# Sending expert rows to their tokens' places in a four-layer Trainium2 kernel, and summing over partitions with PE

## The reference

```python
# layer 2, x here is cond, 1024 x 256
probs = softmax(x @ gate_weight.T)                  # 8 experts
top_v, top_i = top_k(probs, 2);  top_v = top_v / top_v.sum(-1)
for each expert: gate, up = split(x @ gu.T);  y = (silu(gate) * up) @ dp.T
                 out += combine_w[:, e] * y
# layer 3
def weight_quant(w):                                # each of w1, w2, w3
    scale = 1.0 / clip(mean(abs(w)), EPS, None)
    return clip(round(w * scale), -1, 1) / scale
h = silu(bitlinear(x, w1)) * bitlinear(x, w2);  out = bitlinear(h, w3)
```

## Time and profile before

| what | us |
|---|---|
| three runs | 579.07, 580.73, 581.8 |
| median of them | 580.73 |
| the profiled execution's own time | 580.15 |
| its span | 578.4 |
| block loop, first gate_up to last `yb` | 338.7 to 498.6 |
| `yb` of the last block to the last add_y | 498.6 to 525.0 |
| layer 3 behind that | 525.0 to 578.4 |

### The profile page before, as it was taken

One profiled execution on the slowest core, in us unless ns is written; L12 is line 12 of the kernel. 1 busy time (PEld: TensorE's weight loads), 2 busy tenths in 40 slices (PEclk: granted clock), 3 DMA queues, 4 the chain that ended last, 5 costly groups with the idle time before them and its releaser, 6 DMA issues.

```text
span 578.4 us, 6195 instructions
## 1 busy us (share of the span) xinstructions
PE 409.8 (71%) x1772; PEld 265.3 (46%) x1779; DVE 400.1 (69%) x674; ACT 264.2 (46%) x638; POOL 244.4 (42%) x318
## 2 busy tenths in 40 slices
PE   0002599989799999866777259985998999410796
PEld 0001378756455656544556125643555565310464
DVE  4999938698999999997964717558376410153795
ACT  2411164678577777626784103321232323214694
POOL 4666600152985655852300223248156230264342
PEclk9999999999899999988896559999899999855898
DMA  7600000011011100000002197866888895130011
GB/s 245 267 0 1 1 19 1 2 36 38 0 36 38 35 3 19 2 0 1 2 1 74 53 368 260 288 221 228 302 266 323 304 319 195 47 91 27 0 37 36
DMA packets 19408, 60.48 MB, mean 105 GB/s; under 512 B 3024, under 2 KB 8400, under 8 KB 15792
## 3 DMA queue, kind: packets, MB, share of 16 engines
q1 hardware_dynamic: 17504, 54.99, 26.5%
q0 software_dynamic: 1872, 5.11, 3.7%
HBM read 54.98 MB, written 5.11 MB: 104 GB/s over the span
## 4 chain that ended last, share of the span: by engine, by line
PE 41%; DVE 32%; issue 10%; ACT 8%; DMA 4%; POOL 4%; SPq 0%; DVEq 0%; ACTq 0%; POOLq 0%
PE bank L1701 12%; PE bank L1721 6%; DVE fw L887 5%; DVE fw L875 5%; PE bank L1513 4%; DVE bw L878 3%; PE bank L1457 2%; DVE hx L1064 2%; PE bank L1391 2%; ACT rl L636 2%; DMA xb<-cond_rows,row_i 2%; PE bank L1393 2%; PE bank L1392 2%; POOL gy L480 2%; PE bank L1502 2%
## 5 line engine op out<-in xcount | busy, mean ns | idle before, releaser
L1701 PE MATMUL bank<-gu,xbT 128*128 128x512 f32 x184 | 88.4, 626 | 9.0 <-issue 8.1
L636 ACT ACTIVATE rl<-bank,cw 128x128 f32<-128x128 f32 x256 | 73.0, 379 | 38.1 <-DVE hx L1064 21.1
L1513 PE MATMUL bank<-hT,w2raw 128*128 128x512 f32 x128 | 67.8, 613 | 15.1 <-ACT hT L643 15.0
L1267 DVE TENSOR_TENSOR hm<-bank,sl 128x512 f32<-128x512 f32 x23 | 15.8, 687 | 73.6 <-PE bank L1701 42.3
L356 POOL TENSOR_TENSOR fw<-fw,bw 128x256 f32<-128x256 f32 x48 | 38.3, 798 | 53.6 <-DVE bw L878 53.6
L1403 PE MATMUL bank<-ident,GT 128*128 128x128 f32 x64 | 11.8, 340 | 66.4 <-DVE GT L892 45.6
L1701 PEld LDWEIGHTS bank<-gu,xbT 128*128 128x128 f32 x184 | 36.6, 201 | 47.7 <-issue 45.2
L887 DVE RECIPROCAL fw<-fw 128x256 f32<-128x256 f32 x32 | 55.8, 1743 | 0.6
L353 POOL TENSOR_TENSOR eu<-eu,kT 128x256 f32<-128x256 f32 x24 | 25.3, 1055 | 56.2 <-ACT eu L544 49.3
L1064 DVE SCALAR_TENSOR_TENSOR hx<-bank,rl 128x512 f32<-128x512 f32 x64 | 43.4, 680 | 7.7 <-ACT rl L636 7.3
L1721 PE MATMUL bank<-dn,hT 128*128 128x256 f32 x184 | 45.1, 388 | 3.3 <-ACT hT L759 0.7
(11 more groups left out here) (257 smaller groups left out, 878.6 us busy)
## 6 DMA issues: line engine op xcount, KB each, us to landing
gu<-in_gu SPq DMA_DIRECT2D x23, 1024.0 KB, 7.3
dn<-in_dn SPq DMA_DIRECT2D x23, 512.0 KB, 5.3
traw<-in_t SPq DMA_DIRECT2D x3, 1024.0 KB, 4.9
y_rows<-yb SPq DMA_DIRECT2D x23, 128.0 KB, 4.8
w1raw<-in_w SPq DMA_DIRECT2D x8, 256.0 KB, 3.4
w2raw<-in_w SPq DMA_DIRECT2D x8, 256.0 KB, 3.1
kT<-in_kt SPq DMA_DIRECT2D x4, 256.0 KB, 7.5
x<-in_x SPq DMA_DIRECT2D x2, 512.0 KB, 7.1
```

The lines of the kernel that those rows point to most:

```text
L636: ins = act.activation(rl[:, j % 2, e * P:e * P + P], bank[j][:, e * P:e * P + P], ACT.Relu, scale=cw0[:, t, 4 * eg + e:4 * eg + e + 1])
L1513: pe.matmul(bank[4 + o % 2][:], w2raw[:, slot, e, :], hT[:, e % 2, :], start=start, stop=stop, skip_group_check=True).then_inc(sem("y_done ...
L1701: ins = pe.matmul(bank[2 * (b % 2) + up][:], xbT[:, b % 2, k, :], gu[:, b % RING, k, up * I2:up * I2 + I2], start=(k == 0), stop=(k == KC ...
```

## The change

Four things. (1) `owner_i` is worked out before the slots instead of behind them, and SP holds back the weights of block 1 until the first gather has landed and those of block 2 until the second has. (2) The result of a block is no longer stored by SP in slot order but by POOL with an indirect DMA, each row to the place k * 1024 + token of its copy and token (`scatter_block`, two iterations behind); slots that no token has go to rows of their own. For that `tile_no` runs over 16 numbers instead of twice 8, `row_i` takes one DVE instruction more, and two more give `dest_i` (in place of `slot_i`). (3) Behind the loop SP reads `y_rows` back in order, 8 plain DMAs of 256 KB into a buffer of 2 MB that lies over the weights' buffers; DVE waits for two of them per pair of tiles. (4) The ternary sums over partitions are a PE matmul of one column with a matrix of ones, ahead of gate_up of blocks 4, 10 and 16, in a bank which the second half of that gate_up overwrites once DVE has read it; DVE's `ternary_round` moves from the end of its iterations 4, 10 and 16 to their start.

```diff
@@ SP
             for b in range(NB):
+                if 0 < b < RING:
+                    sp.wait_ge(sem(f"xb_in{b - 1}"), 16)
                 block_weights(b)
-                if b >= RING:
-                    block_out(b - RING)
                 if b in (1, 8, 14):
                     ternary_in((1, 8, 14).index(b))
-            for b in range(NB - RING, NB):
-                block_out(b)
+            sp.wait_ge(sem("y_out0"), 16 * ((NB + 1) // 2))
+            sp.wait_ge(sem("y_out1"), 16 * (NB // 2))
+            for b in range(B):
+                for k in range(2):
+                    rows_k = y_d[k * TOK + 2 * P * b:k * TOK + 2 * P * b + 2 * P, :]
+                    sp.dma_start(gy[:, b, k, :, :], rows_k.rearrange("(t p) c -> p t c", p=P)).then_inc(sem(f"gy_in{b}"), 16)
@@ POOL
+            def scatter_block(b):
+
+                pool.wait_ge(sem("y_ready"), b + 1)
+                pool.indirect_dma_start(y_d, bass.IndirectOffsetOnAxis(ap=dest_i[:, b:b + 1], axis=0), yb[:, b % 2, :], None
+                                        ).then_inc(sem(f"y_out{b % 2}"), 16)
...
             for b in range(NB):
                 if b + RING < NB:
                     gather_block(b + RING)
+                if b == 2:
+                    pool.wait_ge(sem("routed"), ROUTED["dest"])
+                if b >= 2:
+                    scatter_block(b - 2)
                 if b < 2 * NBLK:
                     late_sum(b // 2, 1 - b % 2, ("den", "num")[b % 2])
...
-                if b in (3, 9, 15):
-                    ternary_total((3, 9, 15).index(b))
                 if b in (6, 12, 18):
                     ternary_write((6, 12, 18).index(b))
@@ DVE
+            wide = [P, NBW, E2]
+            chain(dve.tensor_tensor(owner[:], slab[:].rearrange("p (j o) -> p j o", o=1).to_broadcast(wide),
+                                    nblk[:, 1, :].rearrange("p (o e) -> p o e", o=1).to_broadcast(wide), ALU.is_ge))
+            chain(dve.tensor_reduce(owner_f[:, 0, :], owner[:], AX.X, ALU.add))
+            dve.tensor_scalar(owner_i[:], owner_f[:, 0, :], float(E2 - 1), None, ALU.min).then_inc(sem("routed"), 1)
             chain(dve.tensor_tensor(nblk[:, 2, :], nblk[:, 1, :], nblk[:, 0, :], ALU.subtract))
...
-            dve.tensor_scalar(row_i[:], row_f[:, 1, :], 0.0, None, ALU.max).then_inc(sem("routed"), 1)
-            dve.tensor_copy(slot_i[:], slots[:, 0, :, :]).then_inc(sem("routed"), 1)
+            chain(dve.tensor_scalar(row_f[:, 2, :], row_f[:, 1, :], float(TOK), -float(TOK), ALU.is_ge, ALU.mult))
+            dve.scalar_tensor_tensor(out=row_i[:], in0=row_f[:, 1, :], scalar=0.0, in1=row_f[:, 2, :],
+                                     op0=ALU.max, op1=ALU.add).then_inc(sem("routed"), 1)
...
             def ternary_round(m):
                 dve.wait_ge(sem("tsum_ready"), m + 1)
-                chain(dve.tensor_scalar(ws[:, 15 + m:16 + m], ws[:, 12 + m:13 + m], 1.0 / (C * HID), 1e-5, ALU.mult, ALU.max))
+                dve.tensor_scalar(ws[:, 15 + m:16 + m], total_bank(4 + 6 * m), 1.0 / (C * HID), 1e-5, ALU.mult, ALU.max
+                                  ).then_inc(sem("tsum_read"), 1)
+                dve.wait_ge(sem("tsum_read"), m + 1)
@@ PE
+            def ternary_total(m):
+                pe.wait_ge(sem("tsum_part"), m + 1)
+                pe.matmul(total_bank(4 + 6 * m), ones[:], ws[:, 9 + m:10 + m], start=True, stop=True).then_inc(sem("tsum_ready"), 1)
...
                 wait(pe, sem("hm_ready"), b - 1)
+                if b in (4, 10, 16):
+                    ternary_total((4, 10, 16).index(b))
                 for up in range(2):
+                    if up and b in (4, 10, 16):
+                        pe.wait_ge(sem("tsum_read"), (4, 10, 16).index(b) + 1)
```

More of the change, by code:

```diff
@@ L45 @@
 ROUTED_SCALE = 2.5
-ROUTED = {"mk": 1, "lsub": 2, "owner": 3, "rows": 4, "slot": 5}
+ROUTED = {"mk": 1, "lsub": 2, "owner": 3, "rows": 4, "dest": 5}
 SUMMED = {"logit": 1, "place": 2, "rows": 3}
@@ L122, in build @@
         ones8 = sb("ones8", [P, E2])
+        ones = sb("ones", [P, P])
         lane1 = sb("lane1", [P, 1])
+        spare = sb("spare", [P, NBW])
         region = cursor[0]
@@ L151, in build @@
         region2 = cursor[0]
+        cursor[0] = region
+        gy = sb("gy", [P, B, 2, 2, C])
+        assert cursor[0] <= region2
+        cursor[0] = region2
         sl = sb("sl", [P, 2, I2])
@@ L173, in build @@
         yb = sb("yb", [P, 2, C])
-        gy = sb("gy", [P, RING, C])
         rtraw = sb("rtraw", [P, KC, E2])
@@ L327, in _ @@
             pool.memset(ones8[:], 1.0).then_inc(sem("route_consts"), 1)
+            pool.memset(ones[:], 1.0).then_inc(sem("route_consts"), 1)
             pool.memset(mk[:], 0.0).then_inc(sem("route_consts"), 1)
@@ L470, in _ @@
                         late_value(b // 2 + 1)
[L471 to L472 removed]
                 if b in (6, 12, 18):
                     ternary_write((6, 12, 18).index(b))
[L477 to L489 removed]
+            scatter_block(NB - 2)
+            scatter_block(NB - 1)
             def rms_stats(mean_sq, root, absmax, out, sum_name, max_name, n, out_name):
@@ L1211, in _ @@
                 dve.tensor_scalar(lane_of[:, i, :], lane[:], lane_no[:, i:i + 1], None, ALU.is_equal).then_inc(sem("lane_ready"), 1)
-            wide = [P, NBW, E2]
-            chain(dve.tensor_tensor(owner[:], slab[:].rearrange("p (j o) -> p j o", o=1).to_broadcast(wide),
-                                    nblk[:, 1, :].rearrange("p (o e) -> p o e", o=1).to_broadcast(wide), ALU.is_ge))
-            chain(dve.tensor_reduce(owner_f[:, 0, :], owner[:], AX.X, ALU.add))
-            dve.tensor_scalar(owner_i[:], owner_f[:, 0, :], float(E2 - 1), None, ALU.min).then_inc(sem("routed"), 1)
             dve.wait_ge(sem("summed"), SUMMED["rows"])
@@ L1280, in _ @@
             for b in range(NB):
+                if b in (4, 10, 16):
+                    ternary_round((4, 10, 16).index(b))
                 if b < 2 * NBLK:
@@ L1295, in _ @@
                     ternary_sum((2, 8, 14).index(b))
-                if b in (4, 10, 16):
-                    ternary_round((4, 10, 16).index(b))
                 if b in (5, 11, 17):
@@ L1303, in add_y @@
                 for k in range(2):
-                    i = 2 * t + k
-                    dve.wait_ge(sem(f"xb_in{i % RING}"), 16 * (len(range(i % RING, NB, RING)) + i // RING + 1))
                     if k:
-                        dve.wait_ge(sem("y_added"), i)
-                    ins = dve.scalar_tensor_tensor(out=x[:, t, :], in0=gy[:, i % RING, :], scalar=cw2p[:, k, t:t + 1], in1=x[:, t, :],
+                        dve.wait_ge(sem("y_added"), 2 * t + 1)
+                    else:
+                        dve.wait_ge(sem(f"gy_in{t // 2}"), 32)
+                    ins = dve.scalar_tensor_tensor(out=x[:, t, :], in0=gy[:, t // 2, k, t % 2, :], scalar=cw2p[:, k, t:t + 1], in1=x[:, t, :],
                                                    op0=ALU.mult, op1=ALU.add)
```

41 lines of the change are left out of this document (14 added, 27 removed).

## The result

The changed kernel takes **553.1 us** (median of 4 runs, 552.6 to 554.94) against 579.9 us for the kernel before (4 runs, 578.93 to 581.8): a ratio of 0.953, 95% interval 0.950 to 0.956. Forecast was 555.3 us, with a range of 549 to 565. The profiled execution of after took 553.12 us (span 551.2), that of before 580.15 (span 578.4).

A forecast was written before the change was run, and what follows sets the result against it. PE bounds the block loop at 6.18 us a block, besides a slow first gather, POOL reduction stalls and the way back. 4.4 + 13.3 - 1.2 + 8.9 = 25.4 us gained, forecast 555.3 us, range 549 to 565.

The forecast's parts named there:

- Stalls, 13.3 us: Block loop: waits around POOL's three ternary reductions vanish with them; 13.3 us gained, 9.3 at the bad end.
- the rival of loads that stay late behind `traw`: Blocks 9 and 15: `traw` still delays gu, 2 us per place, giving 559.3 us; chance 0.12.
- The forecast's sign of it: In the profile after: only one pair of POOL configuration changes left, at the early reduction.
- Totals on PE, 1.2 us lost: PE in the loop: three one-column matmuls at 0.4 us each, 1.2 us lost, between 0 and 3.6.
- Owners and hold, 4.4 us: Start: first gather issued 0.8 us later but landing in 3.3; 4.4 us gained, ends 4.9 gained and 1.3 lost.
- The other rival, a gather that is slow of itself: Start: first gather slow for its own reason, 0.8 us worse instead of 4.4 better, giving 560.5 us; chance 0.10.
- Stores on POOL, nothing lost: Block loop: 23 store issues of 0.98 us fit POOL's 6.18 us per block; nothing lost, 0 to 0.4.
- The pace rival: Block loop: scattered stores landing slower than 11.8 us set the pace; 600 us at 16 us landing; chance 0.04.
- Way back, 8.9 us: Behind the loop: last add at 516.1 instead of 525.01 through plain loads; 8.9 us gained, ends 10.5 and 5.0.
- The forecast's sum of the bad ends: Whole kernel: all unknown costs at their bad ends at once, 12.1 us gained in all, 568.6 us.

The follow-up runs named there:

- x1: Kernel before with only the ternary sums over partitions moved to PE and DVE's rounding moved to iteration starts; 566.32 us, ratio 0.978.
- x9: Changed kernel with each block's result stored a second time by indirect DMA into a tensor nobody reads; 556.38 us, ratio 0.956.
- x5: Changed kernel with the ternary sums over partitions put back on POOL; 582.65 us, ratio 1.002 to the kernel before.
- x6: Kernel before with every ternary reduction on POOL issued twice in a row, the second result unread; 584.13 us, ratio 1.005.
- x7: Kernel before with only SP's two waits holding back weights of blocks 1 and 2, owners still last; 580.06 us, ratio 0.993.
- x2: Kernel before with only owners first and the weights of blocks 1 and 2 held back; 577.13 us, ratio 0.994.
- x4: Changed kernel without SP's two waits that hold back weights, owners still first; 555.61 us, ratio 0.960 to the kernel before.
- x3: Kernel before with only the scattered stores by POOL and the plain loads behind the loop; 585.65 us, ratio 1.008.
- x8: Changed kernel with one `yb` buffer instead of two, each ACT copy waiting for the store before it; 563.77 us (one run).
- x11: Changed kernel with gu of block 1 issued right behind dn of block 0 instead of held back; 553.81 us, ratio 0.954 to before.
- x12: Changed kernel with gu of block 1 not held back and 3 dummy matmuls on PE ahead of the first gate_up; 552.41 us, ratio 0.951.
- x10: Changed kernel with unread dummy matmuls on PE ahead of the first gate_up and of layer 3's first matmuls; 553.43 us, ratio 0.951.

## Why the prediction was right, and where it was off

- **Stalls, 13.3 us.** Right, and on its mechanism: x1 alone brings the loop to 124.30. The trace after has none left, so the rival of loads that stay late behind `traw` falls: gu of block 9, 16.8 us earlier than before, holds nobody up. The room is not wide: in the change this load has 10.64 us until its gate_up at 390.15, in x1 9.43 us are enough (383.69 to 393.12), and in x9, beside twice the stores, 10.15 were too few. That POOL's empty stretches go with the reduction is shown by x1 and x5. That they belong to the configuration and not to the reduction's own work is what x6's second reduction of 0.46 speaks for. The forecast's sign of it came too: line L399, the early reduction, is the only one left with a pair of configuration changes. The 13.3 themselves are those of one execution; the loops of before, x7 and x2 say that the stalls vary by 4.6.
- **Totals on PE, 1.2 us lost.** 20 x 6.18 and three times 0.22 are 124.3, what the loop takes. So each costs 0.22, as the two transposes it was held against, with no wait besides; 0.66 in all.
- **Owners and hold, 4.4 us.** 3.9 of it came: issue 0.63 later (0.8 taken), landing 4.04 (3.3 taken, 2.8 plus 0.5). The gather's issue alone is 1.7 us here, 0.7 above the median of the earlier trace rows where I had put 0.5 on top; the rest of the miss, 0.5, is the landing, which was not as short as the best of the loop. The other rival, a gather that is slow of itself, falls with 3.80 to 4.21 in each of the kernels with both halves. Held-back gu of block 1 was issued at 333.63 (334.0 forecast).
- **Unforecast: 1.0 us in block 0.** Its gate_up takes 5.41 instead of 6.45. The granted clock was 0.50 at its beginning in both; then, over the rest of it, 0.60 before (341.0 to 345.1) and 0.77 after (336.0 to 339.5). PE's idle time ahead of it fell from 10 to 5 us, but over the twelve kernels without dummies it took 5.04 to 6.45 with either idle time (5.04 in x4, behind a gather of 7.89 us; 6.26 in x5, behind one of 4.07), so the cause is open.
- **Stores on POOL, nothing lost.** True for the change and false for the step as it stands in the text. It was worked out from POOL's 6.18 us per block, with the empty stretches already gone, and did not say so. x3 shows the price where they stay: 12.5 us, more than the way back gives. This is a term that depends on another term. The pace rival (deciding from 11.8 us) falls with 5.6 in the middle and 8.2 at worst in x8; 6.3 was taken. By the Trainium skill's rule on the shared port pair ("SBUF — State Buffer", section "SBUF: two separate sides"), GpSimd can't write a DMA's descriptors while DVE runs in a mode that takes the pair. The store's issue takes 0.97 to 2.00 us with a median of 1.00, a spread about as large as that of the gathers, and the loop doesn't feel it; no run ties the slow ones to DVE.
- **Way back, 8.9 us.** 8.9, from errors that cancel, which is luck. The last store landed in 2.43 (2.8 taken); the estimate of 2.3 by the Trainium skill ("DMA: Bandwidth & Descriptors", section "Anatomy of one DMA — SWDGE (gpsimd) path") was nearer. SP's loads land in 4.5 us in the middle and not 3.4; why is open, since the eight loads of the earlier trace rows are as large. Still the first add comes 6.16 behind the last `yb` (6.9 taken), as the first pair lands sooner than the rest. Then DVE waits 0.57 once, which the forecast had excluded, the stretch between the two groups of eight adds takes 3.2 and not 2.8, and the adds follow each other at 0.47 to 0.48 rather than 0.49.
- **The sum.** 25.4 forecast; 27.0 measured by the two profiled executions' times (27.2 by their spans, which the terms add up to) and 26.8 by the medians. The forecast of 555.3 also started from 580.73, the median of three runs; with the fourth it is 579.9. Term by term: start 3.9 for 4.4, block 0 1.0 for nothing, loop 12.6 for 12.1 (13.3 less 1.2), way back 8.9 for 8.9, and 0.8 of run variation ahead and behind. So the mechanism of each large term held, and the closeness of the sum is in part luck: a miss of 0.5 at the start stands against 0.5 in the loop and an unforecast 1.0. The forecast's sum of the bad ends takes the start at 1.4 gained, where its own text has 1.3 lost with a landing of 9.0; with that the bad end would be 571.3 and not 568.6.

What the sum hides: the parts don't add. By the medians beside their own runs of before, x1 gains 15.0 us, x2 4.2, and x3 loses 4.3: 14.9 together. The change gains 26.8. The other 12 are about what x3 loses beyond its way back (8.7 + 4.3 = 13.0): with the totals on PE there is no gap for a store to stand behind.

## What to carry to other kernels

Before costing work that is put on an engine, ask what else that engine does just ahead of it; in x3 a store behind a 10 us gap was a 10 us late store, and with two buffers it became a stall of another engine. Find the piece that frees the shared engine first: here it alone brings more than half of the gain and makes the stores on POOL worth having, and undoing it alone takes back everything. The first gather, which others wait for, got its speed here from both an order (the weights needed first leave early) and a hold (the others leave late), and neither alone did much.

## What the runs showed of the hardware that I had not expected

- In the loop, a reduction over partitions has 6.05 to 9.51 us of empty POOL ahead of its 0.40 us of work and 8.06 to 11.53 behind it, over the 18 in the six kernels that kept it there (before, x2, x3, x5, x6, x7); the same sum by a one-column matmul with ones costs PE 0.22. The same reduction again behind the first is 0.46. The Trainium skill, "GPSIMD Engine Reference", section "2.1 Instruction dispatch", says that the first call of a freshly loaded POOL routine, behind MODIFY_POOL_CONFIG, pays about 6 us (5.95) of code loading that the profile shows as no instruction. That fits the kind of gap. Nearest in size is the early reduction of the kernel before (L388, at 134.34), with 5.67 ahead and 6.95 behind while the DMA engines move 0 and 4 GB/s; the gaps in the loop stand beside 222 to 374 GB/s and are 0.1 to 5.6 longer than the page's figure. Traffic may be the reason, but no run changes it alone, and 6.55 beside 338 GB/s speaks against a simple rule. The gap behind says that something like it is paid on the way back too.
- The same gather of 128 rows lands in 3.8 to 4.2 us, or 7.0 to 8.5 when 1.5 to 5.5 MB of plain loads were issued close to it: 7.89 even where those were issued 2.0 to 6.3 us ahead (x4). With 2.5 MB issued 4.6 to 6.3 us ahead it still landed in 4.05 (x11).
- The time of the first gate_up differs by 1.4 us between kernels that do the same ahead of it, and a burst of dummy matmuls that ends 1.2 us early had lost its effect in one execution (x12) where one that ends in time kept it (x10).
